# Attention and a recurrence on one NeuronCore: the recurrence's product moved ahead of the value products in TensorE's step

## The chip, the cores and the metric

The kernel runs on one core of one Trainium2 chip. Its time is the device time of one execution in microseconds (us); of several executions the median is given. The profile is that of one execution, whose own time is given beside it.

## The reference, cut to what matters

Two branches work on the same normalised input and are added to it:

```python
x = L0_attn_x                       # (2, 1024, 128)
xn = _layernorm(x, axis=-1)
x = x + recurrent_branch(xn) + attention_branch(xn)
```

The recurrent branch is a time mix (three projections k, v, r of a shifted and mixed layer norm, an exponentially weighted running average over the 1024 steps of time) and then a channel mix:

```python
x = x + r * y                                       # y: the running average
h2 = _layer_norm(x, ln2_g, ln2_b)                   # products with a matrix of 1/128: mean, var
ck = h2 * cmix_k + hp2 * (1.0 - cmix_k)
cr = h2 * cmix_r + hp2 * (1.0 - cmix_r)
kk = jnp.square(jax.nn.relu(ck @ w_ck))             # ck0 to ck3
x = x + jax.nn.sigmoid(cr @ w_cr) * (kk @ w_cv)     # cr, cv
```

The attention branch has 16 heads of 8 dimensions over 1024 positions for each of two sequences, with query, key, value and output weights that a gate mixes from experts:

```python
attn = softmax(einsum('bhsd,bhtd->bhst', q, k), axis=-1)
ctx = einsum('bhst,bhtd->bhsd', attn, v)
out = _svd_moe(ctx, oWm, oU, oS, oV, ob, top_idx, gates)
```

## The kernel before, in words

Each engine has a program of its own, written out by hand, and the engines meet through semaphores alone. After an opening of some 63 us (normalising, the gate, the weights, q and k in three bf16 parts) all five engines run the same loop: `PAIRS` = 16 pairs of heads times `KEY_TILES` = 8 tiles of 128 keys, 128 steps in all, numbered 0 to 127 here.

**TensorE's step** (`one_step`, line 1503) issues, in this order: two *fills* ahead (`fill_place`, line 1376), the *scores* of the step's key tile for two halves of 512 queries (`scores`, 8 matmuls, line 1485), two fills behind, the *value products* of the step before (`values`, line 1490), in step 5 of a pair the turning of the maxima (`turn_max`, line 1396), and last the *job* of the step, if it has one (`product`, line 1441). A fill multiplies queries with keys for a later pair of heads, so that VectorE can take the row maximum; the maxima then go into the scores as a row. The value products are four fp32 matmuls with 32 output columns, side by side in the array and accumulated over a pair's eight steps in bank 4 (`PV_BANK`).

**The ring.** Fills and jobs share three PSUM banks in turn (5, 6, 7). Each entry of the list `ring` waits until the entry three places before it has been read:

```python
        def ring_bank(at):
            return bank(A_BANK + at % 3)
...
                dst = ring_bank(at)
                pe.wait_ge(*released(at - 3))
```

In the list a job stands behind the four fills of its step, so three before it is the second fill ahead; three before the next step's first fill behind is the job itself. A fill is released by VectorE's maximum (`read_place`, L1198, semaphore `a_read`), a job by whoever reads it: VectorE for "mean" (L1162) and "cv" (L1167), ScalarE for "var" (L956), "cr" (L979), "ck0" to "ck3" (L974), "mixed" and "values" (L884, L869).

**The jobs.** The recurrence is worked through in four quarters, 26 steps apart (`PRODUCT_STEP`): mean, var, cr, ck0 to ck3 and cv, 32 jobs, each four fp32 matmuls with 32 output columns (16 for cv; L1449). Five leftovers of the opening stand in steps 2, 3, 9, 10 and 15 (L1349 and L1341, over the full array), and two parts of the output ("out", L1428 and L1436) in steps 122 and 125. These 39 of the 128 steps have a job. The fills end with step 116.

**VectorE's step** reads the four fills, then does its part of the recurrence (scans, L1144), and near the end normalises the contexts (L1178, L1180) and adds the outputs (L1190). **ScalarE's step** (`exps`, L985) takes the exponentials of the two halves of scores, in step 0 of a pair copies the finished context of the pair before out of bank 4 (`copy_ctx`, L991, waits for all its value products), and then its part of the recurrence, the reads of jobs among it. SyncE stores each context in DRAM (L457) and, in the last pair, loads those of the second sequence back (L492, L495). GpSimd does most of the elementwise work of the recurrence. ScalarE, VectorE, GpSimd and SyncE take their instructions in the written order.

After the loop TensorE waits for `final_ready` (line 1531, the second output that VectorE has added) and then makes the last output tiles.

Of the kernel before, what the change touches and what calls it, by code (L numbers as in the profile page):

```python
# [62 lines left out]
def build(nc, x, cols, mats, rows, gw1, gb1, gw2, gb2, out):  # L63
# [4 lines left out]
    with ctx:  # L68
# [286 lines left out]
        def flat(t):  # L355
            return t[:, :, :].rearrange("p b t -> p (b t)")

        def place_of(u):

            return u % 2, u // 4, u // 2 % 2  # L360
# [9 lines left out]
        for step in range(STEPS):  # L370
            groups = []
            for half in range(2):
                ahead, unit = divmod(LEAD_UNITS + 2 * (step % KEY_TILES) + half, UNITS)
                n = step // KEY_TILES + 1 + ahead
                at = len(ring)
# [3 lines left out]
            at = len(ring)  # L379
# [3 lines left out]
        def ring_bank(at):  # L383
            return bank(A_BANK + at % 3)
# [5 lines left out]
        def released(at):  # L390

            kind, name, q = ring[at]
            if kind == "place":
                return a_read, filled(at)
            taken_by = {"mean": (centred2, q + 1), "var": (log_var_q, q + 1), "cr": (cr_step, 2 * q + 1),
                        "cv": (gated, q + 1), "mixed": (kvr_read, q + 1), "values": (v_read, q + 1), "out": (final_ready, q + 1)}
            return taken_by[name] if name in taken_by else (relu_ready, q * 4 + int(name[2:]) + 1)
# [841 lines left out]
        def _(pe):  # L1239
# [96 lines left out]
            def values_of(n, dst):  # L1336

                pe.wait_ge(weff_ready, 3)
                for k in range(CHUNK // P):
                    at = CHUNK * (n % 2) + P * k  # L1340
                    last = mm(dst[:, P * k:P * k + P], xnT[:, n // 2, at:at + P], w_eff[:, 2, n // 2, :],  # L1341
                              start=True, stop=True)
                last.then_inc(v_ps, 1)

            def mix_product(m, dst):

                pe.wait_ge(rest_in, 16)
                pe.wait_ge(h_mixed, m + 1)
                mm(dst, mat("t" + "kvr"[m % 3]), mix_slot[m], start=True, stop=True).then_inc(kvr_ps, 1)  # L1349
# [26 lines left out]
            def fill_place(at):  # L1376

                _, n, k = ring[at]
                s, dst = n % SETS, ring_bank(at)
                if at >= 3:  # L1380
                    pe.wait_ge(*released(at - 3))
                e, c, h = place_of(k)
                if n == 0 and k == 0:
                    pe.wait_ge(q_rows_kept, 2)
                    pe.wait_ge(k_rows_kept, 2)
                elif n > 0 and k < 2:
                    pe.wait_ge(main_in[s][e], (n // SETS + (s > 0)) * 96)
                mm(dst, q_main[HALF * e:HALF * (e + 1), s, P * c:P * c + P],  # L1388
                   k_main[HALF * e:HALF * (e + 1), s, CHUNK * h:CHUNK * h + CHUNK],
                   start=True, stop=True).then_inc(a_ready, 1)  # L1390
# [34 lines left out]
            def turn_rt(n, dst, tiles=range(CHUNK // P)):  # L1425

                for at, k in enumerate(tiles):
                    mm(dst[:, P * at:P * at + P], columns_of(RT, n)[:, P * k:P * k + P], ident[:, :],  # L1428
                       start=(at == 0), stop=False)

            def project_ctx(n, dst, tiles=range(CHUNK // P)):

                rows = P if n < 2 else EARLY
                pe.wait_ge(attn_ready, n + 1)
                for at, k in enumerate(tiles):
                    last = mm(dst[:, P * at:P * at + P], ctx_out_T[n][0:rows, P * k:P * k + P],  # L1436
                              w_eff[0:rows, 3, n // 2, :], start=False, stop=(n < 2 and k == 3))
                if n < 2:
                    last.then_inc(final_ps, 1)

            def product(at):

                _, name, q = ring[at]
                dst = ring_bank(at)
                pe.wait_ge(*released(at - 3))

                def columns(weights, moving, start=True, stop=True):
                    for g in range(0, P, 32):
                        last = mm(dst[g:g + 32, :], weights[:, g:g + 32], moving, start=start, stop=stop)  # L1449
                    return last  # L1450

                if name == "mixed":
                    mix_product(q, dst)
                elif name == "values":
                    values_of(q, dst)
                elif name == "out":
                    pe.wait_ge(rt_ready, 2 * q + 2)
                    turn_rt(q, dst)
                    project_ctx(q, dst)
                elif name == "mean":  # L1460
                    pe.wait_ge(x1_ready, q + 1)
                    columns(mean_w, flat(x1)).then_inc(mean2_ps, 1)
                elif name == "var":
                    pe.wait_ge(squared2, q + 1)
                    columns(mean_w, flat(sq2)).then_inc(var2_ps, 1)
                elif name == "cr":
                    pe.wait_ge(mixed, q * 2 + 1)
                    columns(mat("cr"), flat(mix_in[0])).then_inc(cr_ps, 1)
                elif name == "cv":
                    for i in range(4):  # L1470
                        pe.wait_ge(kk_ready, q * 4 + i + 1)
                        last = columns(mat(f"cv{i}"), flat(kk[i]), start=(i == 0), stop=(i == 3))
                    last.then_inc(cv_ps, 1)
                else:
                    pe.wait_ge(mixed, q * 2 + 2)
                    columns(mat(name), flat(mix_in[1])).then_inc(ck_ps, 1)
# [26 lines left out]
            def one_step(p, step):  # L1503

                s, (ahead, behind, jobs) = p % SETS, step_ring[p * KEY_TILES + step]
                for at in ahead:
                    fill_place(at)
                if step == 0:
                    pe.wait_ge(tail_in[p % 2], (p // 2 + 1) * 64)
                    pe.wait_ge(max_in[p % 2], (p // 2 + 1) * 16 * PARTS)  # L1510
                scores(p, s, step, 0)
                scores(p, s, step, 1)
                for at in behind:
                    fill_place(at)
                if step == 1:
                    pe.wait_ge(v_in[p % 2], (p // 2 + 1) * 16)
                    pe.wait_ge(ctx_copied, p + 1)
                if step == TURN_STEP + 1 and p + 1 < PAIRS:
                    pe.wait_ge(turn_read, p + 2)
                if step > 0:  # L1520
                    values(p, s, step - 1)
                elif p > 0:
                    values(p - 1, (p - 1) % SETS, KEY_TILES - 1)
                if step == TURN_STEP and p + 1 < PAIRS:
                    turn_max(p + 1)
                for at in jobs:
                    product(at)

            program(one_step)
            pe.wait_ge(rt_ready, QUARTERS)  # L1530
# [73 lines left out]
```

## Time and profile before

| | |
|---|---|
| median of 3 runs | 443.77 us (442.76 to 444.37) |
| the profiled execution | 443.83 us |
| its span, first to last instruction | 441.7 us |
| TensorE busy (matmuls) | 423.2 us, 96% |
| VectorE busy | 382.5 us, 87% |
| ScalarE busy | 341.7 us, 77% |
| GpSimd busy | 191.6 us, 43% |
| mean granted TensorE clock | 1.000 of full speed |

The profile is of one execution. PE is TensorE's matmuls, PEld its weight loads, DVE is VectorE, ACT ScalarE, POOL GpSimd, SP SyncE (SPq: its DMA issues). The span leaves out 2.1 us of the execution's own time. In a timeline a row is one instruction or a run of like ones on an engine (x4: four), with its start in us from the span's start, its length, and in brackets how long the engine had been idle before it and who ended that.

### The profile page before, as it was taken

The page shows a single profiled execution, that of the slowest core. Times are in us where ns is not written, and L with a number is a line of the kernel's source. Part 1 is how long each engine was busy: PE and PEld are TensorE (multiplying, and loading weights), DVE is VectorE, ACT ScalarE, POOL GpSimd, SP SyncE. Part 2 cuts the span into 40 slices and gives each one's busy share as a digit, 9 for nine tenths or more (in the row PEclk, how much of TensorE's full clock was granted, in tenths as well). Part 3 has the DMA queues.
Part 4 walks back from the last instruction along what each step waited for, and adds up shares of the span by engine and source line. Part 5 has one row for each costly group of instructions (what it writes and reads, how often), then busy time and mean ns, then how long its engine had stood idle before and what let it go on. Part 6 is the DMA issues. An engine that isn't in the chain of part 4 may idle for free.

```text
span 441.7 us, 8603 instructions
## 1 busy us (share of the span) xinstructions
PE 423.2 (96%) x3266; PEld 146.3 (33%) x3266; DVE 382.5 (87%) x657; ACT 341.7 (77%) x466; POOL 191.6 (43%) x271
## 2 busy tenths in 40 slices
PE   1999989999999999999999999999999999999997
PEld 1744222334233222233223322323333332332335
DVE  8469899998999998799999789999978998978182
ACT  3447837879887898788799869878986987898572
POOL 5039681935551625382352537506363620423200
PEclk9999999999999999999999999999999999999999
DMA  6004403141414151404242422333332322050311
GB/s 242 12 7 54 48 7 33 20 67 19 64 22 68 19 67 17 65 9 68 24 62 22 64 23 46 40 53 32 52 36 25 54 26 45 3 130 5 108 47 50
DMA packets 45797, 20.46 MB, mean 46 GB/s; under 512 B 36828, under 2 KB 37500, under 8 KB 45756
## 3 DMA queue, kind: packets, MB, share of 16 engines
q1 hardware_dynamic: 44630, 18.96, 27.7%
q10 hardware_dynamic: 1126, 0.95, 0.6%
q8 instruction: 26, 0.43, 0.4%
q14 instruction: 15, 0.12, 0.1%
HBM read 4.74 MB, written 4.98 MB: 22 GB/s over the span
## 4 chain that ended last, share of the span: by engine, by line
PE 87%; DVE 8%; ACT 3%; issue 1%; DMA 1%; DVEq 0%
PE banks L1498 27%; PE banks L1485 22%; PE banks L1388 18%; PE banks L1449 8%; DVE half_max L1198 5%; PE banks L1349 3%; ACT probs L985 2%; PE banks L1245 1%; PE banks L1428 1%; PE banks L1355 1%; PE banks L1284 1%; PE banks L1436 1%; PE banks L1341 1%; PE banks L1250 1%; DVE stats L1044 1%
## 5 line engine op out<-in xcount | busy, mean ns | idle before, releaser
L1198 DVE TENSOR_REDUCE half_max<-banks 128x1 f32<-128x512 f32 x512 | 318.4, 683 | 19.0 <-PE banks L1388 17.2
L985 ACT ACTIVATE probs<-banks 128x1024 f32<-128x1024 f32 x256 | 248.2, 1023 | 51.5 <-PE banks L1485 48.3
L1498 PE MATMUL banks<-probs,v_op 128*32 128x512 f32 x1024 | 136.4, 605 | 0.0
L1388 PE MATMUL banks<-k_main,q_main 64*128 64x512 bf16 x512 | 117.0, 384 | 5.1 <-DVE half_max L1198 3.3
L1485 PE MATMUL banks<-q_main,k_main 64*128 64x512 bf16 x512 | 99.3, 377 | 0.4 <-ACT probs L985 0.2
L1485 PE MATMUL banks<-q_tail,k_tail 35*128 35x512 bf16 x512 | 99.3, 377 | 0.0
L1388 PEld LDWEIGHTS banks<-k_main,q_main 64*128 64x128 bf16 x512 | 36.7, 93 | 150.2 <-DVE half_max L1198 131.9
L1485 PEld LDWEIGHTS banks<-q_tail,k_tail 35*128 35x128 bf16 x512 | 27.1, 94 | 26.2
L1485 PEld LDWEIGHTS banks<-q_main,k_main 64*128 64x128 bf16 x512 | 26.4, 95 | 25.1 <-ACT probs L985 10.2
L1498 PEld LDWEIGHTS banks<-probs,v_op 128*32 128x32 f32 x1024 | 20.1, 108 | 31.3 <-issue 30.3
L731 POOL TENSOR_TENSOR work<-work 128x512 f32<-128x512 f32 x16 | 16.7, 1041 | 28.6 <-ACT work L974 28.6
L1449 PE MATMUL banks<-hT,mat_sb 128*32 128x512 f32 x160 | 20.9, 592 | 0.0
L726 POOL TENSOR_TENSOR hT<-hT,run 128x512 f32<-128x512 f32 x8 | 9.5, 1193 | 18.5 <-ACT hT L963 18.5
L633 POOL CAST max_op<-max_left 128x16 bf16<-128x16 f32 x16 | 3.2, 198 | 32.9 <-DVE max_left L1203 32.7
L665 POOL TENSOR_TENSOR work<-run 128x512 f32<-128x512 f32 x4 | 4.2, 1041 | 29.0 <-DVE run L1144 29.0
L739 POOL TENSOR_TENSOR RT<-hT,xn_tok 128x256 f32<-128x256 f32 x8 | 5.7, 740 | 21.7 <-DVE xn_tok L1167 21.7
L1449 PE MATMUL banks<-work,mat_sb 128*32 128x512 f32 x128 | 14.5, 592 | 0.0
L706 POOL TENSOR_TENSOR hT<-hT 128x512 f32<-128x512 f32 x4 | 4.2, 1041 | 21.8 <-DVE hT L1162 21.8
L1178 DVE RECIPROCAL parts<-parts 128x512 f32<-128x512 f32 (+1 forms) x4 | 13.3, 3338 | 0.2 <-DMA parts<-ctx_dram 0.2
L1250 PE MATMUL banks<-ident,xn_tok 128*128 128x128 f32 x16 | 4.3, 433 | 9.1 <-DVE xn_tok L1037 9.1
L974 ACT ACTIVATE work<-banks 128x512 f32<-128x512 f32 x16 | 9.6, 599 | 4.3 <-PE banks L1449 4.3
L1167 DVE TENSOR_TENSOR xn_tok<-banks,xn_tok 128x512 f32<-128x512 f32 x4 | 2.8, 692 | 10.7 <-PE banks L1449 10.7
(186 smaller groups left out, 422.3 us busy)
## 6 DMA issues: line engine op xcount, KB each, us to landing
ctx_dram<-ctx_sb SPq DMA_DIRECT2D x15, 256.0 KB, 2.0
q_main<-parts SPq DMA_DIRECT2D x60, 48.0 KB
k_main<-parts SPq DMA_DIRECT2D x60, 48.0 KB
mat_sb<-in_mats_dram SPq DMA_DIRECT2D x2, 768.0 KB, 5.2
v_op<-V SPq DMA_DIRECT2D x16, 64.0 KB, 3.9
parts<-ctx_dram SPq DMA_DIRECT2D x4, 256.0 KB, 4.4
q_main<-parts SPq DMA_DIRECT2D x30, 32.0 KB
k_main<-parts SPq DMA_DIRECT2D x30, 32.0 KB
```

The source lines that it names most:

```text
L726: g.tensor_tensor(mix_in[i][:, :, :], mix_in[i][:, :, :], h2[:, :, 0:QT], ALU.add).then_inc(mixed, 1)
L731: g.tensor_tensor(kk[i][:, :, :], kk[i][:, :, :], kk[i][:, :, :], ALU.mult).then_inc(kk_ready, 1)
L974: a.activation(flat(kk[i]), ring_bank(ring.index(("job", f"ck{i}", q))), ACT.Relu).then_inc(relu_ready, 1)
L985: a.activation(probs[:, (2 * step + h) % 4, :, :], banks[:, 2 * h:2 * h + 2, :], ACT.Exp).then_inc(b_read, 1)
L1178: v.reciprocal(den_T[0:rows, n, :], den_T[0:rows, n, :]).then_inc(recip_ready, 1)
L1198: v.tensor_reduce(half_max[:, n % 2, u:u + 1], ring_bank(at), axis=AX.X, op=ALU.max).then_inc(a_read, 1)
L1250: last = nc.tensor.transpose(token_tiles(bank(n))[:, k, :], xn_tok[:, 4 * n + k, :], ident[:, :])
L1349: mm(dst, mat("t" + "kvr"[m % 3]), mix_slot[m], start=True, stop=True).then_inc(kvr_ps, 1)
L1388: mm(dst, q_main[HALF * e:HALF * (e + 1), s, P * c:P * c + P], k_main[HALF * e:HALF * (e + 1), s, CHUNK * h:CHUNK * h + CHUNK], start=True ...
L1449: last = mm(dst[g:g + 32, :], weights[:, g:g + 32], moving, start=start, stop=stop)
L1485: last = mm(bank(2 * h + e), k_rows[HALF * e:HALF * e + used, at, P * step:P * step + P], q_rows[HALF * e:HALF * e + used, at, CHUNK * h:C ...
L1498: last = mm(banks[g:g + 32, PV_BANK, :], v_op[:, s % 2, step, e, :], probs[:, (2 * step + h) % 4, e, :], start=(step == 0), stop=True, ski ...
```

## The change

Inside TensorE's step the job is issued before the value products and the turning of the maxima instead of after them. The list `ring`, its banks and the waits of every entry stay as they are, and so do the programs of the four other engines.

```diff
@@ -1512,6 +1512,8 @@
                 scores(p, s, step, 1)
                 for at in behind:
                     fill_place(at)
+                for at in jobs:
+                    product(at)
                 if step == 1:
                     pe.wait_ge(v_in[p % 2], (p // 2 + 1) * 16)
                     pe.wait_ge(ctx_copied, p + 1)
@@ -1523,8 +1525,6 @@
                     values(p - 1, (p - 1) % SETS, KEY_TILES - 1)
                 if step == TURN_STEP and p + 1 < PAIRS:
                     turn_max(p + 1)
-                for at in jobs:
-                    product(at)
```

TensorE's order in step 39 (job ck3 of the first quarter), with the waits of each instruction; L1388 are fills, L1498 the value products, L1449 the job, L1485 the scores of step 40:

```order
 L1388 MATMUL banks<-k_main,q_main 128x512 [waits relu_ready]
 L1388 MATMUL banks<-k_main,q_main 128x512 [waits a_read]
-L1498 MATMUL banks<-probs,v_op 32x512 [waits b_read]
-L1498 MATMUL banks<-probs,v_op 32x512 x3
-L1449 MATMUL banks<-hT,mat_sb 32x512 [waits mixed,a_read]
-L1449 MATMUL banks<-hT,mat_sb 32x512 x3
+L1449 MATMUL banks<-hT,mat_sb 32x512 [waits mixed,a_read]
+L1449 MATMUL banks<-hT,mat_sb 32x512 x3
+L1498 MATMUL banks<-probs,v_op 32x512 [waits b_read]
+L1498 MATMUL banks<-probs,v_op 32x512 x3
 L1388 MATMUL banks<-k_main,q_main 128x512 [waits a_read] x2
 L1485 MATMUL banks<-q_main,k_main 128x512 [waits b_read,max_in1,tail_in1]
```

The job now follows the fills behind directly, and the value products stand between it and the next step's fills. So it is in every step with a job.

TensorE's order in step 120 (job cv of the last quarter, 16 matmuls; the value products are the last of a pair). Before:

```order
L1485 MATMUL banks<-q_tail,k_tail 128x512 x2
L1498 MATMUL banks<-probs,v_op 32x512 [waits b_read]
L1498 MATMUL banks<-probs,v_op 32x512 x3
L1449 MATMUL banks<-work,mat_sb 32x512 [waits kk_ready,a_read]
L1449 MATMUL banks<-work,mat_sb 32x512 x3
L1449 MATMUL banks<-work,mat_sb 32x512 [waits kk_ready]
```

With the change:

```order
L1449 MATMUL banks<-work,mat_sb 32x512 [waits kk_ready]
L1449 MATMUL banks<-work,mat_sb 32x512 x3
L1498 MATMUL banks<-probs,v_op 32x512 [waits b_read]
L1498 MATMUL banks<-probs,v_op 32x512 x3
L1485 MATMUL banks<-q_main,k_main 128x512 [waits b_read]
```

The value products that close the pair stand behind all 16 matmuls of the job here.

ScalarE's order in step 64 and at the start of step 65, which stays as it was; L991 waits for the value products that close a pair (`pv_done`), L974 reads the job ck2:

```order
L985 ACTIVATE probs<-banks 128x1024 [waits b_ready] x2
L991 COPY ctx_sb<-banks 128x512 [waits ctx_out1,pv_done]
L942 ACTIVATE xn_tok<-run 128x512 [waits sum_ready]
L974 ACTIVATE work<-banks 128x512 [waits ck_ps]
L985 ACTIVATE probs<-banks 128x1024 [waits b_ready] x2
```

Nothing moved here, but what L991 waits for and what L974 waits for have changed places on TensorE.

## Rows read from the trace of the kernel before

**Rows 1.** The page: busy times, and a group with its mean and its idle time

```profile
PE 423.2 (96%) x3266; PEld 146.3 (33%) x3266; DVE 382.5 (87%) x657; ACT 341.7 (77%) x466; POOL 191.6 (43%) x271
...
L1198 DVE TENSOR_REDUCE half_max<-banks 128x1 f32<-128x512 f32 x512 | 318.4, 683 | 19.0 <-PE banks L1388 17.2
```

**Rows 2.** Timeline of TensorE's matmuls, step 51, which has no job

```profile
207.11 1.06 PE L1498 MATMUL banks<-probs,v_op 128*32 128x512 f32 x8
208.11 0.39 PE L1388 MATMUL banks<-k_main,q_main 64*128 64x512 bf16 x2
```

**Rows 3.** Timeline of step 39 (job ck3): TensorE, its weight loads, VectorE, ScalarE

```profile
173.42 0.39 PE L1388 MATMUL banks<-k_main,q_main 64*128 64x512 bf16 x2
173.84 2.48 DVE L1198 TENSOR_REDUCE half_max<-banks 128x1 f32<-128x512 f32 x4 [0.86 <-PE banks L1388]
174.52 0.46 PE L1388 MATMUL banks<-k_main,q_main 64*128 64x512 bf16 x2
174.59 0.09 PEld L1388 LDWEIGHTS banks<-k_main,q_main 64*128 64x128 bf16 x1 [0.19 <-DVE half_max L1198]
174.91 1.07 PE L1498 MATMUL banks<-probs,v_op 128*32 128x512 f32 x8
175.37 0.13 PEld L1449 LDWEIGHTS banks<-hT,mat_sb 128*32 128x32 f32 x4 [0.30 <-DVE half_max L1198]
175.79 1.04 PE L1449 MATMUL banks<-hT,mat_sb 128*32 128x512 f32 x8
176.77 0.39 PE L1388 MATMUL banks<-k_main,q_main 64*128 64x512 bf16 x2
176.90 0.60 ACT L974 ACTIVATE work<-banks 128x512 f32<-128x512 f32 x1 [0.68 <-PE banks L1449]
```

**Rows 4.** Timeline of step 54 (job var): what GpSimd squares for it, and TensorE

```profile
216.00 1.04 POOL L706 TENSOR_TENSOR hT<-hT 128x512 f32<-128x512 f32 x1
219.16 1.04 PE L1449 MATMUL banks<-hT,mean_w 128*32 128x512 f32 x8
```

**Rows 5.** Timeline of steps 78 and 79 (job mean)

```profile
289.87 0.69 DVE L1162 TENSOR_TENSOR hT<-hT,banks 128x512 f32<-128x512 f32 x1 [0.57 <-PE banks L1449]
290.83 0.77 PE L1388 MATMUL banks<-k_main,q_main 64*128 64x512 bf16 x2
```

**Rows 6.** Timeline of steps 42 and 43 (job cv)

```profile
187.87 0.69 DVE L1167 TENSOR_TENSOR xn_tok<-banks,xn_tok 128x512 f32<-128x512 f32 x1 [1.92 <-PE banks L1449]
188.76 0.84 PE L1388 MATMUL banks<-k_main,q_main 64*128 64x512 bf16 x2
```

**Rows 7.** Timeline of ScalarE in steps 64 and 65, and TensorE's values and fills

```profile
247.30 1.06 PE L1498 MATMUL banks<-probs,v_op 128*32 128x512 f32 x8
248.50 0.59 ACT L991 COPY ctx_sb<-banks 128x512 f32<-128x512 f32 x1
...
249.50 0.61 ACT L974 ACTIVATE work<-banks 128x512 f32<-128x512 f32 x1
250.26 0.46 PE L1388 MATMUL banks<-k_main,q_main 64*128 64x512 bf16 x2
```

**Rows 8.** Timeline from step 120 to the end of the loop, all engines

```profile
408.09 1.07 PE L1498 MATMUL banks<-probs,v_op 128*32 128x512 f32 x8
408.97 3.62 PE L1449 MATMUL banks<-work,mat_sb 128*32 128x512 f32 x32
409.59 0.59 ACT L991 COPY ctx_sb<-banks 128x512 f32<-128x512 f32 x1
412.52 0.39 PE L1485 MATMUL banks<-q_main,k_main 64*128 64x512 bf16 x2
419.78 3.35 DVE L1178 RECIPROCAL parts<-parts 112x512 f32<-112x512 f32 x1 [0.24 <-DMA parts<-ctx_dram]
428.38 0.69 DVE L1190 TENSOR_TENSOR x_sb<-x_sb,banks 128x512 f32<-128x512 f32 x1
430.99 1.16 PE L1428 MATMUL banks<-ident,RT 128*128 128x128 f32 x8
```

## The prediction

> **What bounds the kernel now.** I read the page first, then the timeline of TensorE and VectorE side by side for single steps, with and without a job, then the places where something else than TensorE comes last. By the page TensorE is busy for 96% of the span and VectorE for 87% [rows 1], so neither can lose much without the end moving. A step without a job shows how they are tied: the value products start at 207.11 and the next fills at 208.11, 1.00 us later [rows 2], and the reader should see in [rows 3] what comes between one pair of fills and the next. The fills ahead start at 173.42, VectorE begins to read at 173.84, 0.42 later, and reads four banks in 2.48 us. With 0.68 for one read [rows 1], the reads start (2.48 - 0.68) / 3 = 0.60 apart. The first ends at 173.84 + 0.68 = 174.52, and at 174.59 the weights of the second fill behind are loaded: a release takes 0.07 us to reach TensorE. So TensorE already waits for VectorE in the middle of every step.
>
> In a step with a job TensorE is the slower one. From fill to fill it takes 176.77 - 173.42 = 3.35 us, VectorE 2.48 and then nothing to do: it stood idle for 0.86 before its first read [rows 3]. Whatever TensorE waits for in such a step is therefore added to the time; VectorE has no backlog in which it could vanish.
>
> **The change, part by part.** No instruction is added or removed, and no other engine's order changes. TensorE's job and value products change places in 39 steps.
>
> *The product's wait.* The job needs the bank of the second fill ahead. VectorE's second read ends at 173.84 + 0.60 + 0.68 = 175.12, the release arrives at 175.19. Before, the job's turn came at 175.79 and it found the bank free. Now its turn comes where the value products stood, at 174.91 [rows 3]. It waits 175.19 - 174.91 = 0.28, say 0.29 us with rounding, and the value products behind it wait too, though nothing holds them (TensorE takes matmuls in order). After it the sum of the two is the same: job and values take 0.88 and 0.98 in either order [rows 3]. All four-fill steps with a job have this shape: 39 less the two last ck, the last cv and the two output jobs, which have no fills behind and whose bank is free, so 34. **34 x 0.29 = +9.9 us.** From below: without the 0.07 of the release 34 x 0.21 = 7.1. From above: the first weight load of the job lay under the value matmuls (175.37 against 175.79, [rows 3]) and may now stand in the open after the wait, 0.13 at most by the same rows, 34 x 0.13 = 4.4 more. I take 0.29, because the second fill behind is a case of exactly this kind, a matmul that waits with its weight load, and it is the nearest row. For the five jobs over the full array I take the same; no row shows that order of shapes.
>
> VectorE's reads start 0.60 apart though one lasts 0.68 [rows 1, 3]. The Trainium skill ("VectorE: DVE Perf Modes", section "The DRAIN you can't avoid") says that the next operation does not start until the pipe is empty, which would put the second release at least 0.08 later: 34 x 0.08 = 2.7 us more, some 456. The trace contradicts it for these reads, so the sum goes by 0.60, and the rule has no chance of its own beside rival C, which ends near the same time.
>
> *Do the job's inputs arrive?* The tightest is var: GpSimd's square ends at 217.04, the job started at 219.16 [rows 4] and now would at 218.56. Nothing waits there.
>
> *Where the product's reader was late.* VectorE reads "mean" 1.11 us after the job starts (289.87; TensorE's step has the times of [rows 3]) and thereby delays its own first read: the next step's fills behind took 0.77 instead of 0.46 [rows 3, 5]. The job now starts 0.88 - 0.29 = 0.59 earlier and the next fills come 0.29 later, so VectorE is done in time: 4 x 0.31 = **-1.2 us**. For "cv" 0.84 against 0.46 [rows 3, 6], three times (the fourth has no fills behind it): 3 x 0.38 = **-1.1 us**.
>
> *What waits for the value products.* Only ScalarE's copy of the finished context (L991), in step 0 of a pair, and it has a queue behind it. Jobs fall on such steps at 64, 80, 88, 104 and 120. In step 64 the copy starts at 248.50, 1.20 after the values at 247.30, and L974, which reads the job, at 249.50 [rows 7]. The values would now start at 247.30 + 0.29 + 0.88 = 248.47, and a product of that kind is seen by its reader 1.11 later [rows 3], at 249.58. So everything on ScalarE moves by 1.08: L974 starts at 250.58 and ends at 251.19, with 0.07 at 251.26. The next step's first fill behind needs that bank, at 250.26 + 0.29 = 250.55 [rows 7], and waits 0.71. That step has a job too, whose wait of 0.29 and the 0.07 between its two fills fall inside, so 0.35 is left. The same in step 88; in 80 the reader of var comes 0.5 earlier in the queue, and some 0.2 is left; in 104 VectorE reads the job, nothing. **+0.9 us**; from below 0, from above 2 x 0.71 + 0.3 = 1.7.
>
> *The end.* In step 120 the job is cv: 412.52 - 408.97 = 3.55 us [rows 8]. The last values but one pair, at 408.09, go behind it: 408.09 + 3.55 - 0.10 (the 0.98 and 0.88 above) = 411.54, seen at 412.65 instead of 409.59, where L991 started. Behind this copy hangs a chain through DRAM: SyncE stores and loads, VectorE's reciprocal at 419.78 had waited for that load, and its addition L1190 ends at 428.38 + 0.69 = 429.07 [rows 8]. TensorE waits for that addition after the loop and was there at 430.99. With 3.06 more it is 432.13, with 0.07 432.20: a new wait of 1.2. **+1.2 us**; from below 0, from above 1.2 plus as much again if the loads now meet the store of the first output. SyncE's other waits (stage of values, maxima) move by up to 1.2 us and have the rest of a pair's eight steps as cover. The turning of the maxima stays behind the value products in steps 37, 61 and 117 and only comes 0.3 later, with ScalarE's copy of it still ahead of the next exponentials.
>
> **The sum:** 9.9 - 1.2 - 1.1 + 0.9 + 1.2 = +9.7 us. Against the profiled execution's 443.83, which is 0.06 over the median, that gives **453.5 us**, 2.2% slower.
>
> **The rivals.**
>
> *A. The earlier product is worth having (441.5).* If the bank were free when the job's turn comes, only the gains would be left: 443.83 - 1.2 - 1.1 = 441.5. That needs the second read to end 0.28 earlier than 175.12 [rows 3]. For it: in seven steps a reader on VectorE was late. Against it: the reads are tied to the fills ahead, 0.42 and 0.60 later each, and no row shows them sooner. Chance 3%.
>
> *B. Much of it is given back (447.4).* The wait is there, but the next step's own wait for VectorE (0.19 before the second fill behind, [rows 3]) shrinks by as much: 34 x 0.18 = 6.1 less. Against it: that wait runs from the fills ahead, which move with TensorE. Chance 6%.
>
> *C. The wait is dearer (457.5).* The job's weight load stands in the open after the release, or the switch to four column tiles does: 453.5 + 4.4 = 457.9, at half of it 455.7. For it: the values' own first load stands at 174.91 with them, not ahead of them, behind the fill that waited. Against it: the second fill behind starts with its load in the same row. The Trainium skill ("TensorE: Matmul & The Clock Gate", section "Step-by-step: what each phase is for") says that weight loads are pulled ahead of running matmuls while matmuls stay in order; by that the value products cannot pass the waiting job, and the load hidden before is the job's, which is this rival. Chance 12%.
>
> *D. The order makes no difference (443.8).* If the moved lines did nothing, or both engines were paced by something else. Against it: the order above shows the job moved in front, and the page leaves 4% of TensorE. Chance 3%.
>
> **How the numbers follow.** My forecast has the remaining 76%: 453.5 us. Its own bounds are 443.83 + 7.1 - 2.3 = 448.6 from below (no ScalarE term, no wait at the end) and 453.5 + 4.4 + 0.8 + 1.2 = 459.9 from above. The range 449.5 to 457.5 holds it but for its ends, and most of C; left out are A, B and D with 12%, and the tails. A measurement of this kernel can tell 0.3%, 1.3 us, from no change. Faster by more than that is A, 3%; within it D, 3%; slower the rest, 94%.
>
> **What would show it.** TensorE waits for VectorE's L1198 before the job in 34 steps, 0.3 us each, and a step with a job takes 3.64 instead of 3.35. Fills behind after mean and cv take 0.46 instead of 0.77 and 0.84. In steps 65 and 89 the first fill behind waits for ScalarE's L974. L991 in step 120 starts 3 us later, and at the end of the loop TensorE waits for L1190. If steps with jobs are no longer than before, the first term is wrong, and with it the sign; if they take 3.75 and more, C is right; if the step after a job is shorter than 2.49, B.

## The result and the profile after

The changed kernel takes **453.01 us**, median of 4 runs (451.85 to 453.15), against 443.88 for the kernel before in the same comparison; the ratio is 1.0196 with an interval of 1.0176 to 1.0216. The forecast of 453.5 us was right. The profiled execution took 453.15 us with a span of 451.0, which is 9.3 us more than before. All profiled executions here were at a granted clock of 1.000 but the one of the job ahead of the fills behind.

Whole executions scatter by over 1 us, and the traces show where: the first scores come at 62.3 to 64.0 us, whatever was edited behind them, while steps that no edit touches agree within 0.02 us from trace to trace. So small terms are read from the steps and not from the medians. The timelines below, like those of the rows ahead of the prediction, are picked lines of longer ones.

The page of the changed kernel, its line of busy times and the group of VectorE's maxima:

```profile
PE 423.7 (94%) x3265; PEld 146.3 (32%) x3266; DVE 383.3 (85%) x657; ACT 340.3 (75%) x466; POOL 191.6 (42%) x271
L1198 DVE TENSOR_REDUCE half_max<-banks 128x1 f32<-128x512 f32 x512 | 318.8, 684 | 29.9 <-PE banks L1388 28.1
```

Against [rows 1] the work is the same, 423.7 us on TensorE and 383.3 on VectorE. The time went into waiting. VectorE now stands idle for 29.9 us before its maxima, 10.9 more than before, and it waits for the fills. That alone doesn't say who is the cause: VectorE waits because TensorE came late, and TensorE was late because it had waited for VectorE. The timeline of step 39 shows it (TensorE, its weight loads, VectorE; compare [rows 3]):

```profile
176.31 0.39 PE L1388 MATMUL banks<-k_main,q_main 64*128 64x512 bf16 x2
176.73 2.48 DVE L1198 TENSOR_REDUCE half_max<-banks 128x1 f32<-128x512 f32 x4 [1.14 <-PE banks L1388]
177.41 0.46 PE L1388 MATMUL banks<-k_main,q_main 64*128 64x512 bf16 x2
178.07 0.16 PEld L1449 LDWEIGHTS banks<-hT,mat_sb 128*32 128x32 f32 x8 [0.50 <-DVE half_max L1198]
178.08 1.06 PE L1449 MATMUL banks<-hT,mat_sb 128*32 128x512 f32 x8 [0.21 <-DVE half_max L1198]
178.53 0.13 PEld L1498 LDWEIGHTS banks<-probs,v_op 128*32 128x32 f32 x4 [0.30 <-ACT probs L985]
178.96 1.04 PE L1498 MATMUL banks<-probs,v_op 128*32 128x512 f32 x8
179.93 0.39 PE L1388 MATMUL banks<-k_main,q_main 64*128 64x512 bf16 x2
```

The second read of VectorE ends at 176.73 + 0.60 + 0.68 = 178.01, and the job starts at 178.08 with a new bracket: idle for 0.21, released by L1198. The value products behind it, which wait for nothing, start at 178.96. From fills to fills the step takes 179.93 - 176.31 = 3.62 us instead of 3.35. In the list of waits the job's entry has grown; before, its weight loads were put down with 8.7 us in 29 waits and its matmuls not at all:

```profile
PEld banks L1449 <- DVE half_max L1198: 13.6, 27, 0.5
PE banks L1449 <- DVE half_max L1198: 5.6, 27, 0.2
```

The first figure is the total, the second the count. 5.6 / 27 = 0.21 us. A wait costs 0.07 more than this idle time, because without it the next matmuls start 0.07 before the recorded end of the fill (in [rows 3] the value products at 174.91, the fill's end at 174.52 + 0.46 = 174.98). 27 are the 34 less the five jobs over the full array, which stand under other lines, and less those of steps 65 and 89, where the wait falls inside a longer one that comes below.

Each step's length in both traces, taken from scores to scores, gives where the 9.3 us are:

| part of the sum | predicted | measured |
|---|---|---|
| the product's wait, 34 steps | 34 x 0.29 = +9.9 | 34 x 0.278 = +9.45 (0.275 to 0.281 in 32 of them) |
| the product's reader late, mean (4) | -1.2 | -1.23 (2.795 to 2.486; 2.844 to 2.537 once) |
| the same, cv (3) | -1.1 | -1.13 (0.376 to 0.380 each) |
| what waits for the value products | +0.9 | +0.86 (steps 65, 89: 0.34 each beyond their own 0.28; step 81: 0.19; step 82: -0.03) |
| step 119, after the turning in 117 | none | -0.14 |
| the end | +1.2 | +1.38 |
| the opening, not changed | 0 | +0.14 |
| **span** | **+9.7** | **+9.3** |

The gains of the two middle rows, in the timelines behind a mean (steps 78 and 79) and behind a cv (steps 42 and 43); in each the product's reader is done before the next fills ahead, and the fills behind take the ordinary 0.46 us:

```profile
294.24 0.69 DVE L1162 TENSOR_TENSOR hT<-hT,banks 128x512 f32<-128x512 f32 x1
...
296.06 0.46 PE L1388 MATMUL banks<-k_main,q_main 64*128 64x512 bf16 x2
```

```profile
186.67 3.64 PE L1449 MATMUL banks<-work,mat_sb 128*32 128x512 f32 x32 [0.21 <-DVE half_max L1198]
190.45 0.69 DVE L1167 TENSOR_TENSOR xn_tok<-banks,xn_tok 128x512 f32<-128x512 f32 x1 [1.34 <-PE banks L1449]
...
192.20 0.46 PE L1388 MATMUL banks<-k_main,q_main 64*128 64x512 bf16 x2
```

They stood at 0.77 and 0.84 in [rows 5, 6]. ScalarE's queue in steps 64 and 65 (compare [rows 7]):

```profile
252.62 1.04 PE L1498 MATMUL banks<-probs,v_op 128*32 128x512 f32 x8
253.72 0.59 ACT L991 COPY ctx_sb<-banks 128x512 f32<-128x512 f32 x1 [0.95 <-PE banks L1498]
...
254.74 0.59 ACT L974 ACTIVATE work<-banks 128x512 f32<-128x512 f32 x1
255.38 0.39 PE L1388 MATMUL banks<-k_main,q_main 64*128 64x512 bf16 x2 [0.53 <-ACT work L974]
```

The copy waits for the late value products, L974 stands behind it though its own product is long finished, and TensorE's fill waits 0.53 for L974. And the end, from step 120 on, all engines (compare [rows 8]):

```profile
416.03 3.64 PE L1449 MATMUL banks<-work,mat_sb 128*32 128x512 f32 x32
419.48 1.04 PE L1498 MATMUL banks<-probs,v_op 128*32 128x512 f32 x8
420.59 0.59 ACT L991 COPY ctx_sb<-banks 128x512 f32<-128x512 f32 x1 [2.95 <-PE banks L1498]
421.20 0.32 SPq L457 DMA_DIRECT2D ctx_dram<-ctx_sb  x1
430.97 3.35 DVE L1178 RECIPROCAL parts<-parts 112x512 f32<-112x512 f32 x1 [4.48 <-DMA parts<-ctx_dram]
439.53 0.67 DVE L1190 TENSOR_TENSOR x_sb<-x_sb,banks 128x512 f32<-128x512 f32 x1
440.34 1.13 PE L1428 MATMUL banks<-ident,RT 128*128 128x128 f32 x8 [1.34 <-DVE x_sb L1190]
```

The reciprocal had waited 0.24 us for its load and now waits 4.48, and TensorE stands idle for 1.34 before its last part, which begins 2.41 behind the value products at 437.93 instead of 1.00: 1.41 late.

### The profile page after: what moved, and what is told of

It is laid out like the page before. It is cut to its first block, busy times and chain, and to the rows that moved or that the text cites. A ratio compares the mean times of both kernels' runs of the same rounds, so it can differ in the third digit from the quotient of the medians.

```text
span 451.0 us, 8602 instructions
## 1 busy us (share of the span) xinstructions
PE 423.7 (94%) x3265; PEld 146.3 (32%) x3266; DVE 383.3 (85%) x657; ACT 340.3 (75%) x466; POOL 191.6 (42%) x271
## 4 chain that ended last, share of the span: by engine, by line
PE 75%; DVE 17%; ACT 2%; DMA 2%; issue 2%; SPq 1%
PE banks L1498 24%; PE banks L1388 15%; PE banks L1485 15%; DVE half_max L1198 13%; PE banks L1449 10%; PE banks L1349 3%; DVE parts L1178 1%; PE banks L1245 1%; ACT probs L985 1%; PE banks L1355 1%; DMA parts<-ctx_dram 1%; PE banks L1284 1%; PE banks L1341 1%; PE banks L1250 1%; DVE stats L1044 1%
## 5 line engine op out<-in xcount | busy, mean ns | idle before, releaser
L1198 DVE TENSOR_REDUCE half_max<-banks 128x1 f32<-128x512 f32 x512 | 318.8, 684 | 29.9 <-PE banks L1388 28.1
L1498 PE MATMUL banks<-probs,v_op 128*32 128x512 f32 x1024 | 135.6, 601 | 0.0
L1388 PE MATMUL banks<-k_main,q_main 64*128 64x512 bf16 x512 | 114.6, 384 | 6.0 <-DVE half_max L1198 3.3
L1485 PE MATMUL banks<-q_main,k_main 64*128 64x512 bf16 x512 | 99.4, 377 | 0.3
L1485 PE MATMUL banks<-q_tail,k_tail 35*128 35x512 bf16 x512 | 99.4, 377 | 0.0
L1388 PEld LDWEIGHTS banks<-k_main,q_main 64*128 64x128 bf16 x512 | 36.4, 93 | 150.4 <-DVE half_max L1198 128.1
L1498 PEld LDWEIGHTS banks<-probs,v_op 128*32 128x32 f32 x1024 | 23.4, 108 | 43.4 <-issue 35.2
L1485 PEld LDWEIGHTS banks<-q_tail,k_tail 35*128 35x128 bf16 x512 | 27.2, 94 | 26.0
L1485 PEld LDWEIGHTS banks<-q_main,k_main 64*128 64x128 bf16 x512 | 26.4, 95 | 26.3 <-ACT probs L985 10.0
L1449 PE MATMUL banks<-hT,mat_sb 128*32 128x512 f32 x160 | 21.3, 605 | 3.3 <-DVE half_max L1198 3.3
L1449 PE MATMUL banks<-work,mat_sb 128*32 128x512 f32 x128 | 14.6, 595 | 0.6 <-DVE half_max L1198 0.6
L991 ACT COPY ctx_sb<-banks 128x512 f32<-128x512 f32 x15 | 8.8, 590 | 7.1 <-PE banks L1498 7.1
L700 POOL TENSOR_TENSOR xn_tok<-xn_tok 128x512 f32<-128x512 f32 x4 | 5.1, 1279 | 13.2 <-ACT xn_tok L953 13.2
```

The lines of the kernel that those rows point to most:

```text
L991: a.copy(ctx_sb[:, s % 2, :], bank(PV_BANK)).then_inc(ctx_copied, 1)
L1198: v.tensor_reduce(half_max[:, n % 2, u:u + 1], ring_bank(at), axis=AX.X, op=ALU.max).then_inc(a_read, 1)
L1485: last = mm(bank(2 * h + e), k_rows[HALF * e:HALF * e + used, at, P * step:P * step + P], q_rows[HALF * e:HALF * e + used, at, CHUNK * h:C ...
L1498: last = mm(banks[g:g + 32, PV_BANK, :], v_op[:, s % 2, step, e, :], probs[:, (2 * step + h) % 4, e, :], start=(step == 0), stop=True, ski ...
```

## The experiments

Two theories stood against each other: the time is the wait for the bank that VectorE's second read releases (mine), or the order of shapes and weight loads itself costs (rival C). Beside them the smaller terms each had a run. "Loop" below is the time from the first scores to those of step 127, against the kernel before.

**A first read of half the length, in the order before.** If the wait is for VectorE's second read, that read must be moved without touching TensorE. In the 34 steps the first maximum reads 256 columns instead of 512; half of that maximum is left out.

```diff
+        short_reads = [ahead[0] for ahead, behind, jobs in step_ring if len(behind) and len(jobs)]
...
-                v.tensor_reduce(half_max[:, n % 2, u:u + 1], ring_bank(at), axis=AX.X, op=ALU.max).then_inc(a_read, 1)
+                src = ring_bank(at)[:, 0:CHUNK // 2] if at in short_reads else ring_bank(at)
+                v.tensor_reduce(half_max[:, n % 2, u:u + 1], src, axis=AX.X, op=ALU.max).then_inc(a_read, 1)
```

> The order of before, but in the 34 steps with four fills and a job VectorE's first read takes 256 of the 512 columns of its bank (half of that maximum is left out), so that the second read and its release come about 0.27 us earlier. It is the control for the next kernel. Bank theory (the job waits for the release of the second fill ahead): only the second fill behind gains, 0.07 to 0.08 a step, a step with a job goes from 3.35 to 3.27, 34 x 0.08 = 2.7 us, 441.2. Theory of shapes (the loss comes from the order of the matmuls and their weight loads, whatever VectorE does): the same here, 441.2.

441.3 us, ratio 0.9946 (0.9926 to 0.9966). A step with a job takes 3.265 instead of 3.347, the loop 2.72 less. This is what the next run is measured against. (The edit moves lines by 3: L1391 fills, L1201 maxima, L1452 jobs, L1501 value products.)

**The same read, in the changed order.**

> The changed order with the same short first read in the same 34 steps. Bank theory: the release of the second fill ahead reaches TensorE at about 1.27 us after the first scores instead of 1.54, against 1.18 at which the job's turn comes, so 0.09 of 0.28 is left, a step takes 3.36 instead of 3.62, and the time falls by some 9 us to 444.2, 3.0 over its control. Theory of shapes: the step keeps 0.28 over its control, 450.3, some 9 over it.

444.64 us, ratio 1.001 (0.9993 to 1.0028): 3.3 above its partner, where my theory asked for 3.0 and shapes for 9. Step 39 of this kernel, TensorE, its loads and VectorE:

```profile
173.75 0.39 PE L1391 MATMUL banks<-k_main,q_main 64*128 64x512 bf16 x2
174.17 2.38 DVE L1201 TENSOR_REDUCE half_max<-banks 128x1 f32<-128x256 f32 x4 [0.98 <-PE banks L1391]
174.85 0.38 PE L1391 MATMUL banks<-k_main,q_main 64*128 64x512 bf16 x2
175.25 1.06 PE L1452 MATMUL banks<-hT,mat_sb 128*32 128x512 f32 x8
175.25 0.16 PEld L1452 LDWEIGHTS banks<-hT,mat_sb 128*32 128x32 f32 x8 [0.50 <-DVE half_max L1201]
177.10 0.39 PE L1391 MATMUL banks<-k_main,q_main 64*128 64x512 bf16 x2
```

The job starts 0.40 after the second fill behind, and its matmuls have no wait in brackets any more. The step takes 3.357 against 3.265 in the partner: what is left of the wait is 0.09, because the second read still ends at 174.17 + 0.34 + 0.68 = 175.19. (0.34 is the distance of its start from the first one's in this trace.) The order of the shapes costs nothing that could be seen beside that. It had little chance to: job and value products have the same shape (128*32 128x512 in the rows above), so in 29 of the 34 steps both orders change shape equally often. Only the five jobs over the full array give another order, and they lose the same 0.276 to 0.280 in the changed kernel. 34 x 0.092 = 3.1 us for the wait, with 1.4 for ScalarE's queue (in steps 65 and 89 it is 0.61 each here, because less of the job's own wait falls inside it) and less the gains behind mean and cv and that of step 119, make the loop's +1.96 over its partner, and 1.1 come at the end. (Steps 42, 35 and 61 differ by 0.03, 0.06 and 0.12 from the partner's instead of 0.09.) The job itself moved with VectorE's read one for one: it starts 1.27 us after the scores instead of 1.54, and the second read 0.27 earlier.

**ScalarE copies the context last.** In the changed order, the copy goes behind ScalarE's part of the recurrence.

```diff
                 exps(p, step)
-                if step == 0 and p > 0:
-                    copy_ctx(p - 1, p - 1, (p - 1) // 2)
                 for t, q in quarters_at(now):
                     branch(t, q)
+                if step == 0 and p > 0:
+                    copy_ctx(p - 1, p - 1, (p - 1) // 2)
```

> The changed order, with ScalarE's copy of the finished context behind its part of the recurrence instead of ahead of it in step 0 of a pair. Queue theory (the copy waits for the later value products and holds up the reads of the jobs behind it): the first fill behind in steps 65 and 89 no longer waits, these steps go from 3.97 to 3.62, step 81 from 2.68 to 2.49, 0.85 us in all, 452.2. Rival (those three steps are late because the job's own wait moved the reads): no change, 453.0.

452.35 us, ratio 1.0203 (1.0177 to 1.0229). The median lies within the scatter of the changed kernel's; the trace is the finer measure, and there steps 65 and 89 take 3.623 instead of 3.969, step 81 is back at 2.486, and the loop is 0.89 us shorter than the changed kernel's, where the term was 0.86. Steps 64 and 65 of this kernel, ScalarE and the fills:

```profile
251.92 0.60 ACT L974 ACTIVATE work<-banks 128x512 f32<-128x512 f32 x1
252.47 0.59 ACT L991 COPY ctx_sb<-banks 128x512 f32<-128x512 f32 x1
253.43 0.46 PE L1388 MATMUL banks<-k_main,q_main 64*128 64x512 bf16 x2
```

The two have changed places and the fill waits for nobody but VectorE, in between its two matmuls as everywhere.

**The last cv goes back behind the value products.** Only step 120 has the order before.

```diff
-                for at in jobs:
+                now = p * KEY_TILES + step
+                early = now != 120
+                for at in jobs if early else ():
                     product(at)
...
+                for at in jobs if not early else ():
+                    product(at)
```

> The changed order everywhere but in step 120, where the job cv of the last quarter stands behind the value products as before. End theory (the context copy of step 120 came 3.1 us later and so did the addition for which TensorE waits after the loop): the wait at the end of the loop goes, 1.4 us less, 451.6, and ScalarE's copy in step 120 starts 2.47 after the scores as before. Rival (the end is longer because the product of the last output comes earlier or loads and store collide): no change, 453.0.

451.82 us, ratio 1.018 (1.0153 to 1.0206), 1.2 below the changed kernel; in the trace the part behind the loop is 1.38 shorter. The copy of the context in step 120 and TensorE's last part in this kernel:

```profile
417.52 0.59 ACT L991 COPY ctx_sb<-banks 128x512 f32<-128x512 f32 x1
...
437.92 1.07 PE L1498 MATMUL banks<-probs,v_op 128*32 128x512 f32 x8
438.92 1.16 PE L1428 MATMUL banks<-ident,RT 128*128 128x128 f32 x8
```

L1428 follows the value products after 1.00 with no wait; in the changed kernel it came 440.34 - 437.93 = 2.41 behind them. So the wait of the end comes from step 120's order, some 24 us earlier.

**VectorE adds the output first.** The other way to take that wait away leaves TensorE alone: in step 125 the addition L1190 goes ahead of the second reciprocal.

```diff
-                if now in NORMALISED:
-                    normalise_ctx(NORMALISED[now])
                 if now in OUT_JOBS:
                     add_out(OUT_JOBS[now], ring_bank(ring.index(("job", "out", OUT_JOBS[now]))))
+                if now in NORMALISED:
+                    normalise_ctx(NORMALISED[now])
```

> The changed order, and in step 125 VectorE adds the second output before it normalises the fourth context instead of behind that (4.4 us of reciprocal and product). End theory: the addition for which TensorE waits after the loop ends some 4 us earlier, no wait is left there, 1.4 us less, 451.6, with the job of step 120 still ahead of the value products. If the wait at the end is for the normalised contexts themselves and not for this addition: no change or a little more, 453.0 to 453.7.

452.45 us, ratio 1.0193 (1.017 to 1.0217). The end of this kernel:

```profile
435.52 0.68 DVE L1190 TENSOR_TENSOR x_sb<-x_sb,banks 128x512 f32<-128x512 f32 x1
436.12 3.34 DVE L1178 RECIPROCAL parts<-parts 112x512 f32<-112x512 f32 x1
438.14 1.06 PE L1498 MATMUL banks<-probs,v_op 128*32 128x512 f32 x8
439.14 1.16 PE L1428 MATMUL banks<-ident,RT 128*128 128x128 f32 x8
```

Again no wait, L1428 1.00 behind the values, and in the trace the 1.38 us of the end are gone. The median is only 0.6 below the changed kernel's, less than expected; with four runs that scatter by over 1 us this comparison can't tell 0.6 from 1.4. The mechanism is shown by the trace, the saving in whole runs is not settled by it.

**Only where a reader was late.** Mean, the first three cv and the ck3 of step 117 go early, all other jobs stay behind the value products; the edit is that of step 120's run with another set of steps.

```diff
+                early = now in (26, 52, 78, 104, 42, 68, 94, 117)
```

> Only eight jobs ahead of the value products: mean of all quarters, cv of the first three, and ck3 of the last (step 117); all others behind them as before. By the sum of the parts as the trace of the change has them: seven steps 0.28 longer (+1.9), four following steps 0.31 and three 0.38 shorter (-2.4), step 119 0.14 shorter: -0.6 us, 443.3, a little under before. If the gain after mean and cv needed the other jobs moved too: +1.9, 445.8.

443.3 us of 12 runs against 444.18 of 17, ratio 0.9983 (0.9967 to 0.9998). In the trace the loop is 0.555 us shorter: 7 x 0.278 for the wait, less 4 x 0.309, 3 x 0.378 and 0.136. Of the kernels that leave nothing out it is the only one that came out ahead of the kernel before, by 0.2%, less than the 0.3% that the prediction took as the limit of such a measurement; the steps show the gain, the medians hardly.

**All but those.** Nearly the complement (step 117 goes early here too, step 120 in neither kernel): `early = now not in (26, 52, 78, 104, 42, 68, 94, 120)`.

> The complement: all jobs ahead of the value products but mean, the first three and the last cv. 27 steps 0.28 longer (7.5), steps 65, 81, 89 by ScalarE's queue 0.86 longer, step 119 0.14 shorter, and none of the gains after mean and cv, none of the wait at the end: +8.2 us, 452.1. If parts did not add up (the wait at the end comes whatever cv of the last quarter does), 453.5.

452.3 us, ratio 1.0184 (1.016 to 1.0209); the loop is 8.23 longer. With the -0.56 of the run before that is 7.67, and since both have the -0.14 of step 117, which must count once only, 7.81. The whole change has 7.80: the parts add up, and no interaction is hidden in the sum.

**The job ahead of the fills behind.** If the wait is for a bank of the ring, a job that takes its place in the ring before the fills behind finds a bank that was free long ago. For mean and the first three cv, TensorE, the list `ring` and VectorE's reads were reordered so.

```diff
+        FIRST = (26, 52, 78, 104, 42, 68, 94)
...
+                if half == 1 and step in FIRST:
+                    at = len(ring)
+                    ring += [("job", name, q) for name, q in jobs_at(step)]
+                    jobs = range(at, len(ring))
...
-                for at in (*step_ring[now][0], *step_ring[now][1]):
+                for at in step_ring[now][0]:
                     read_place(at)
-                for t, q in quarters_at(now):
+                early = [(t, q) for t, q in quarters_at(now) if now in FIRST and t in (PRODUCT_STEP["mean"], PRODUCT_STEP["cv"])]
+                for t, q in early:
                     branch(t, q)
+                for at in step_ring[now][1]:
+                    read_place(at)
...
+                for at in jobs if now in FIRST else ():
+                    product(at)
                 for at in behind:
                     fill_place(at)
```

> An attempt at the early product without its wait: for mean (four) and the first three cv the job stands before the fills behind, in the ring too, and VectorE reads it between the fills ahead and those behind; all others as before. Its bank is then that of the last fill of the step before, long free. Bank theory: no wait for the job, the step 0.04 longer by one more change of shapes and without the wait of the second fill behind, the next step 2.69 instead of 2.80 (mean) and 2.76 instead of 2.86 (cv): -0.5 us, 443.4. Theory of shapes: a step with a job 0.3 longer here too, +1.5, 445.4.

This missed: 454.86 us, ratio 1.0251 (1.0223 to 1.0279), 11.5 over what I expected. The half that it was built on held: the job starts 0.96 to 1.03 us after the scores and waits for no bank. Already there a mean costs +0.16 in its own step, where I expected 0.04 and the theory of shapes 0.3, and gives back 0.12 in the next. And steps 43, 69 and 95 take 5.69, 6.54 and 5.17 us instead of 2.9. The timeline from the end of step 42 on (L1401 fills, L1151 scans, L1205 maxima, L1498 here the scores):

```profile
186.57 1.43 POOL L746 TENSOR_TENSOR RT<-hT,xn_tok 128x256 f32<-128x256 f32 x2 [3.25 <-DVE xn_tok L1174]
187.60 2.54 DVE L1151 TENSOR_TENSOR_SCAN run<-work,run,quarter_in 128x256 f32<-128x256 f32 x2
187.95 1.65 POOL L750 TENSOR_TENSOR x_sb<-x_sb,vb_ob 128x512 f32<-128x512 f32 x1
190.07 2.45 DVE L1205 TENSOR_REDUCE half_max<-banks 128x1 f32<-128x512 f32 x4
190.78 0.39 PE L1401 MATMUL banks<-k_main,q_main 64*128 64x512 bf16 x1 [2.37 <-DVE half_max L1205]
...
192.84 0.63 PE L1498 MATMUL banks<-q_main,k_main 64*128 64x512 bf16 x2
```

The two scans of the recurrence, which VectorE has in the same step as cv, had stood ahead of the late read and filled the time of cv's long product. Now they stood behind the reads of the fills behind, so next to the next step's reads, and TensorE's fill waited 2.37 us for them. Two more things made it worse, and both are told below: the scans took 0.93 and 1.68 us, and TensorE's clock fell.

**The scans go first again.** VectorE does its whole part of the recurrence between the two pairs of reads, scans ahead of cv's read: `early = quarters_at(now) if now in FIRST else []`.

> As the kernel with the early jobs (mean and three cv before the fills behind, read by VectorE between the fills ahead and those behind), but in these steps VectorE does all its part of the recurrence there, the two scans of the next quarter ahead of its read of cv. In the kernel before this one the scans stood behind the late reads and started in the next step, 6.6 us later than usual, and steps 43, 69, 95 took 5.2 to 6.5 us. If the scans' place is the cause of that: steps 43, 69, 95 take 2.75 to 2.8, the loop falls by some 10 us, 444.4, no gain against before, since the job costs 0.16 more there than a job behind the values. If VectorE's late read of cv as such is the cause: steps 43, 69, 95 stay above 5, 454.

444.71 us, ratio 1.0013 (0.9996 to 1.003). (The expectation says that the scans had started 6.6 us later than usual; it is 6.6 us into step 42 instead of 2.6, so 4.0 later.) Steps 43, 69 and 95 take 2.74, 2.78 and 2.73 us. Step 42 of this kernel, VectorE:

```profile
184.94 1.40 DVE L1151 TENSOR_TENSOR_SCAN run<-work,run,quarter_in 128x256 f32<-128x256 f32 x2 [0.87 <-POOL quarter_in L690]
187.39 0.69 DVE L1174 TENSOR_TENSOR xn_tok<-banks,xn_tok 128x512 f32<-128x512 f32 x1 [1.05 <-PE banks L1462]
```

So the long steps were the scans' place and nothing in TensorE's order. What is left is +0.34 in the loop, and it has two parts. The first is TensorE's own, as in step 26 (L1462 the job mean, L1401 fills):

```profile
136.72 1.07 PE L1462 MATMUL banks<-hT,mean_w 128*32 128x512 f32 x8
137.72 0.39 PE L1401 MATMUL banks<-k_main,q_main 64*128 64x512 bf16 x2
...
139.04 0.55 PE L1401 MATMUL banks<-k_main,q_main 64*128 64x512 bf16 x2
```

From the job to the fills it takes 1.00 us, and from the value products behind them, at 138.04, to the next fills 1.00 again, where 0.88 and 0.98 were enough when the two followed each other [rows 3]. TensorE goes from the one shape to the other once more in such a step, and the step is longer by 0.16 with a mean and by 0.17 to 0.23 with a cv, though the job waits for nothing. That the extra change of shape is the cause is argued from this spacing and has no run of its own. The second part: of the 0.31 and 0.38 by which VectorE's late read lengthened the next step only 0.12 and 0.13 come back, because the fills behind are now read later. Even with a free bank the early product doesn't pay.

## Why the prediction was right, step by step

*The product's wait* carried the sum and held to 4%: 0.278 for 0.29, the same within 0.004 in 32 of the 34 steps, the five jobs over the full array among them, which no row had shown (in steps 65 and 89 it falls inside the wait for ScalarE and can't be told apart). I had rounded 0.28 up. The two runs with a short read show the cause and not only the size: with the second read 0.27 earlier, 34 x 0.092 = 3.1 us of its 9.45 are left.

*The Trainium skill's rule on VectorE* ("VectorE: DVE Perf Modes", section "The DRAIN you can't avoid") would have put the second release later, by the sentence that the prediction took from it. The trace goes by 0.60 here as well: the reads of 0.68 us take 2.48 for four, and the job starts 0.07 after the end that this gives. The prediction read only half of that section, which goes on that a next operation that is not held starts earlier; with that half the trace agrees.

*Rival C* fell. The job's first load does stand in the open now, at 178.07, 0.01 ahead of its matmul, but the step is longer by 0.278 and not by 0.41. The rival, and my upper bound with it, had overlooked that the cover is handed on: before, the value products' first load stood in the open and the job's lay under their matmuls [rows 3]; now the value products' load, at 178.53, lies under the job's. One first load stands in the open in either order. What the Trainium skill says of loads that are pulled ahead ("TensorE: Matmul & The Clock Gate", section "Step-by-step: what each phase is for") agrees with both traces, but it isn't a reason for a longer step here. (The rival's own sum was 457.9; the 457.5 of its heading is the end of the range.)

*Where the product's reader was late*: -1.23 and -1.13 for -1.2 and -1.1. *What waits for the value products*: +0.86 for +0.9, and the run with the copy last takes this away (0.89 in its loop). *The end*: 1.38 for 1.2. L991 came 3.06 later against the scores of step 120, as forecast, but the addition L1190 ended 3.19 later: from the store of the context at 421.20 to the reciprocal at 430.97 it took 9.77 us, and before, in its trace, 9.58, of which 0.13 are left at the addition. And TensorE started 0.14 after the addition's end (440.34 against 439.53 + 0.67 = 440.20), where I had taken 0.07.

One term was missing. I had said of the turning of the maxima that it "only comes 0.3 later". In step 117 the opposite end mattered: the job ck3 comes earlier and with it ScalarE's reads, the copy of the maxima is taken at 3.02 us after the scores instead of 3.52, ScalarE's second exponential of step 118 starts 0.13 earlier, and step 119, whose scores wait for it, takes 2.205 instead of 2.343. It is worth -0.14.

*Rival A* needed a free bank, and the bank was late by the full 0.28. *Rival B* needed the step after a job to give something back; those without another cause take 2.486 as before. *Rival D* asked for no change, and the change is 9.1 us.

## What to carry to other kernels

Where banks are handed round in a ring, an instruction's place in the engine's order has to be read together with whose release it needs: work that needs no release, put ahead of the one that does, is cover for it, and moving it behind costs the wait in full. Price a reordering by the release time of each moved instruction against its new turn, then look in every in-order queue downstream (here ScalarE's copy and, behind it, a trip through DRAM that ends 24 us later in a wait of TensorE) for who needs what has been moved back. Where only some of the moved places gain, split the change by place: 8 of the 39 gained, by 0.03 to 0.14 us each; 27 others and the cv of step 120 made the loss, and in steps 116, 122 and 125 the order cost nothing. A reordering that adds a change of shape has to be priced for that too.

## What the runs showed of the hardware

**VectorE and GpSimd held each other up.** In the run with the job first, the second scan took 1.68 us instead of 0.73, the first 0.93 instead of 0.74, and GpSimd's addition L750 1.65 instead of 1.27. The same came in steps 69 and 95, within 0.01 us. The times fit a lock that each in turn had to wait for: the first scan ended at 188.53, so its own 0.74 began at 187.79, 0.21 before the end of GpSimd's L746 (186.57 + 1.43 = 188.00); that addition began at 187.95, and 187.95 + (1.65 - 1.27) = 188.33 is 0.20 before the end of the first scan (187.60 + 0.93 = 188.53); the second scan ended at 190.14, so its own 0.73 began at 189.41, 0.19 before the addition's end at 189.60. The Trainium skill ("SBUF — State Buffer", section "Who interferes with whom") says that a VectorE instruction with two inputs in SBUF and a GpSimd instruction that reads SBUF exclude each other; the trace agrees, for a scan too. With the scans elsewhere L750 takes 1.27 again. That the lock is the cause was not tested by itself.

**TensorE's clock fell after two of three equal stalls.** In the same kernel TensorE had been idle for 2.37 us up to 190.78, up to 270.44 and up to 350.24. Windows behind each (busy us and counts of each engine, then the granted clock):

```profile
190.80:191.60 0.80, 0.80 (x9) 0.23 (x9) 0.80 (x2) 0.00 (x0) 0.80 (x1) 1.00 0.00 0
192.80:194.60 1.80, 1.80 (x12) 0.59 (x8) 1.48 (x3) 0.66 (x1) 0.33 (x1) 0.50 0.00 0
195.20:197.00 1.80, 1.80 (x18) 0.48 (x19) 1.76 (x3) 0.71 (x2) 1.63 (x4) 1.00 0.00 0
270.50:271.30 0.80, 0.80 (x5) 0.24 (x9) 0.80 (x2) 0.00 (x0) 0.80 (x1) 0.50 0.00 0
350.30:352.30 2.00, 2.00 (x17) 0.58 (x19) 2.00 (x4) 0.00 (x0) 2.00 (x2) 1.00 0.00 0
```

In 192.8 to 194.6 the granted clock is 0.50, which is 1.2 GHz, and the scores' matmuls start 0.43 us apart instead of 0.22; from 195.2 on it is back. After the second stall it is at 0.50 at once, after the third it never left 1.00, though the stall was as long and came in the same kind of step; why is not known from these runs. Steps 43 and 44 together took 9.18 us, 69 and 70 9.08, and 95 and 96, at full clock, 7.66, so the low clock cost some 1.5 us each time. In the changed kernel, whose waits are many but short, the clock stayed at 1.000 throughout.

**A shorter read moves the next one by less than its columns.** With 256 columns instead of 512 the next maximum starts 0.34 us after it instead of 0.60. By these two spacings a column costs 0.26 / 256, some 0.001 us, and each read 0.08 beside it, an estimate from two points.
